# A two-layer adaLN and FFN kernel on one core: first w12 rows loaded and turned earlier, other orders of VectorE's and ScalarE's work, fewer self-waits

## What is computed

```python
x = x + L0_ffn(L0_cond(x, cond, ...), gate, kernel, bias, lora_A, lora_B, ...)
x = x + L1_ffn(L1_cond(x, cond, weight, c_weight, fside), w12, b12, w3, b3)
# L0_cond: a 64x64 mixing matrix per batch row, a softmax blend of eight
# L0_ffn:  x @ kernel + bias + two LoRA terms (one gated per group, one shared)
# L1_cond: a grouped conv over the 1024 positions (9 taps, 4 groups of 16 channels) + ctx + bias
# L1_ffn:
x12 = einsum('bsk,mk->bsm', x, w12) + b12        # w12: 2048 x 1024
x1, x2 = split(x12, 2)
x4 = silu(x1) * x2
return einsum('bsm,nm->bsn', x4, w3) + b3        # w3: 1024 x 1024
```

## Time and profile before

| what | us |
|---|---|
| the three timed runs | 838.28, 838.53, 830.34 |
| their median | 838.28 |
| the profiled execution, its own time | 831.89 |
| its span, first to last instruction | 829.8 |
| TensorE's mean granted clock in it | 0.985 of full speed |

### The profile page before, as it was taken

One profiled execution on the slowest core, in us unless ns is written; L12 is line 12 of the kernel. 1 busy time (PEld: TensorE's weight loads), 2 busy tenths in 40 slices (PEclk: granted clock), 3 DMA queues, 4 the chain that ended last, 5 costly groups with the idle time before them and its releaser, 6 DMA issues.

```text
span 829.8 us, 10413 instructions
## 1 busy us (share of the span) xinstructions
PE 786.4 (95%) x3889; PEld 659.2 (79%) x3889; DVE 532.7 (64%) x634; ACT 208.1 (25%) x251; POOL 88.3 (11%) x59
## 2 busy tenths in 40 slices
PE   5998889999999999789999999999999989999998
PEld 4867678888888999668888877877778868888886
DVE  4855775264443479987777759766665795565552
ACT  4431101010010032233333326332233641111110
POOL 4440532323222000000000000000000000000000
PEclk9999999999999999899999999999999999999999
DMA  8966845455455896244455232277754764444441
GB/s 277 238 180 188 216 109 132 122 119 135 111 143 127 199 279 194 70 126 127 126 159 145 76 127 77 64 200 206 203 163 177 271 236 152 153 152 152 167 161 76
DMA packets 88379, 131.45 MB, mean 158 GB/s; under 512 B 11208, under 2 KB 66936, under 8 KB 85656
## 3 DMA queue, kind: packets, MB, share of 16 engines
q1 hardware_dynamic: 85136, 129.90, 53.4%
q10 hardware_dynamic: 3064, 0.90, 0.7%
q0 software_dynamic: 144, 0.21, 0.1%
HBM read 78.20 MB, written 51.72 MB: 157 GB/s over the span
## 4 chain that ended last, share of the span: by engine, by line
PE 72%; DVE 10%; DMA 8%; SPq 5%; issue 3%; ACT 2%; DVEq 0%; ACTq 0%
PE ps L1561 30%; PE ps L1804 25%; PE ps L1862 16%; DMA w_raw<-in_L_ffn_w 2%; DVE cr L1279 1%; DVE cf L1271 1%; SPq L438 1%; DMA w_scratch<-w_d 1%; SPq L592 1%; DMA x<-x_scratch 1%; DVE w_s_lo L1252 1%; DMA lora_b_scratch<-lb_c_lo 1%; DMA h_f<-h_scratch 1%; SPq L355 1%; DMA res<-r_scratch 1%
## 5 line engine op out<-in xcount | busy, mean ns | idle before, releaser
L1804 PE MATMUL ps<-cr,w_s_hi 128*128 128x512 f32 x512 | 159.5, 393 | 5.1 <-ACT s L915 4.9
L1804 PE MATMUL ps<-cr,w_a_hi 128*128 128x512 f32 x384 | 122.2, 400 | 10.7 <-DVE s L1357 6.0
L1804 PEld LDWEIGHTS ps<-cr,w_s_hi 128*128 128x128 f32 x512 | 96.5, 189 | 27.2 <-issue 4.0
L1804 PE MATMUL ps<-cr,w_s_lo 128*128 128x512 f32 x256 | 100.2, 391 | 0.0
L1804 PEld LDWEIGHTS ps<-cr,w_a_hi 128*128 128x128 f32 x384 | 73.3, 192 | 28.4 <-DVE s L1357 8.1
L1561 PE MATMUL ps<-wk_hi,y_hi 128*128 128x512 f32 x256 | 80.5, 395 | 0.3 <-issue 0.3
L1561 PE MATMUL ps<-wk_lo,y_hi 128*128 128x512 f32 x256 | 79.0, 390 | 0.0
L1561 PE MATMUL ps<-wk_hi,y_lo 128*128 128x512 f32 x256 | 78.9, 389 | 0.0
L1127 DVE TENSOR_TENSOR x_t<-ps,x_t 128x1024 f32<-128x1024 f32 x16 | 19.6, 1222 | 92.3 <-PE ps L1561 92.3
L741 POOL TENSOR_TENSOR x_t<-x_in,f_bias 128x1024 f32<-128x1024 f32 x16 | 63.3, 3960 | 143.0 <-DMA x_scratch<-x_t 143.0
L1499 DVE TENSOR_TENSOR res<-ps,res 128x512 f32<-128x512 f32 x56 | 38.6, 689 | 59.0 <-PE ps L1862 58.3
(11 more groups left out here) (176 smaller groups left out, 1255.4 us busy)
## 6 DMA issues: line engine op xcount, KB each, us to landing
x_scratch<-x_t SPq DMA_DIRECT2D x128, 64.5 KB, 2.1
x<-x_scratch SPq DMA_DIRECT2D x32, 258.0 KB, 7.4
x_in<-in_x SPq DMA_DIRECT2D x16, 512.0 KB, 5.3
r_scratch<-r_t SPq DMA_DIRECT2D x16, 512.0 KB, 3.1
raw<-in_L_ffn_w SPq DMA_DIRECT2D x64, 128.0 KB, 4.7
h_scratch<-s SPq DMA_DIRECT2D x32, 256.0 KB, 2.4
h_f<-h_scratch SPq DMA_DIRECT2D x8, 1024.0 KB, 5.9
res<-r_scratch SPq DMA_DIRECT2D x16, 512.0 KB, 5.0
```

Source lines behind the costliest of these rows:

```text
L1804: last = pe.matmul(o, l, r, start=first and q == 0 and n == 0, stop=q == 3 and n == 2, skip_group_check=True)
```

## The change

- The first two w12 loads (prep 0) go to two buffers of their own (`raw_first`, over `la_hi`, free once GpSimd has gathered it) and are issued ahead of `store_x1` of tile 12. VectorE turns them behind the conv's rows 0 and 2, where it was rows 7 and 8, and sums and splits prep 0 earlier. SP's other issues in the conv get a new order (`load_c_bias(1)`, `store_a(0)`, the wait for the stores of r).
- VectorE's sums and low parts of c in the conv stand in another order; c_lo of t3 comes ahead of rows 29 to 31. The self-wait and `c_staged` in `take_c` go; SP waits for `c_taken` itself. TensorE waits for 29 rows ahead of b21 and for all 32 ahead of b22.
- ScalarE's order in a unit: `part_copy` 1 is ahead of the first silu; in units 9 to 14 `a_hi` is ahead of `part_copy` 0.
- Pass change: the operand t1 of pass B gets a new slot 16 (199.75 KB), so that VectorE's `c_sum` for it waits for no product; ScalarE's `silu` stands behind `part_copy` 1 there. raw2 moves to 24 KB, slot 3, its load for unit 9 waits for unit 7's b21.
- Units 9 to 14: `a_lo` is ahead of `s_lo`, w3's turns and first two differences are ahead of `part_add` 1 and the other two behind it. SP's `load_a` is ahead of `store_w3` and waits only for the two `a_lo`.
- Projection head: VectorE makes add 1 and add 2 ahead of the last w3 low part, and h of unit 1 behind add 3.

The diff, cut to what the text speaks of:

```diff
+        SLOT_KB = [8 * n for n in range(16)] + [199.75]
...
-        raw2 = at("w_a_raw", [P, 2, PH, P], 199.75)
+        raw2 = at("w_a_raw", [P, 2, PH, P], 24)
+        raw_first = [at(f"raw_first{s}", [P, NL], 64 + 4 * s) for s in range(2)]
...
-        T3, B22 = operand("t3", 48, 24), operand("b22", 56, 32)
+        T3, B22 = operand("t3", 48, 199.75), operand("b22", 56, 32)
...
-        LO_B, HI_B = dict(zip(PRODUCTS, (14, 1, 5, 3, 4, 12, 8))), dict(zip(PRODUCTS, (13, 9, 6, 7, 15, 10, 11)))
+        LO_B, HI_B = dict(zip(PRODUCTS, (14, 1, 5, 16, 4, 12, 8))), dict(zip(PRODUCTS, (13, 9, 6, 7, 15, 10, 11)))
...
             def load_w12(n):
                 for half in range(2):
-                    if n:
+                    if n > 1:
                         sp.wait_ge(w_free, 2 * n + half - 1)
                     for q in range(4):
-                        dst = raw[half][32 * q:32 * q + 32, :].rearrange("b (m l) -> b m l", m=4)
+                        dst = (raw if n else raw_first)[half][32 * q:32 * q + 32, :].rearrange("b (m l) -> b m l", m=4)
...
                 if n == HALF_UNITS:
-                    sp.wait_ge(w_free, 2 * HALF_UNITS)
+                    sp.wait_ge(g_mm, 7 * HALF_UNITS - 5)
                     sp.wait_ge(a_stored, 16 * (NJ - 2))
                 else:
-                    sp.wait_ge(w_lo_made, 4 * n)
+                    sp.wait_ge(w_lo_made, 4 * n - 2)
...
+            sp.wait_ge(la_gathered, NG)
+            load_w12(0)
             store_x1(TILES - 4, 0, TILES - 1)
             store_x1(TILES - 3, 1, TILES)
...
-            load_c_bias(1)
             for s in range(2):
                 sp.wait_ge(x1_stored[s], 128 * TILES // 2)
             load_x8(4)
             load_x8(5)
+            def store_c(k):
+                sp.wait_ge(c_taken, 8 + 16 + k + 1)
+                sp.dma_start(c_dram[k // 8, :, k % 8, :], c_st[k % 4][:, :]).then_inc(c_stored[k % 4], 16)
+            for t in range(6, 9):
+                load_x8(t)
+            store_a(0)
+            load_x8(9)
+            load_c_bias(1)
+            for t in range(10, 12):
+                load_x8(t)
             for s in range(2):
                 sp.wait_ge(r_stored[s], 16 * TILES // 2)
-            load_w12(0)
-
-            def store_c(k):
-
-                sp.wait_ge(c_staged, k + 1)
-                sp.dma_start(c_dram[k // 8, :, k % 8, :], c_st[k % 4][:, :]).then_inc(c_stored[k % 4], 16)
-
-            for t in range(6, 12):
-                load_x8(t)
-            store_a(0)
             load_w12(1)
...
-                if u == HALF_UNITS - 2:
-                    load_a(HALF_UNITS)
                 if u == HALF_UNITS - 1:
                     sp.wait_ge(g_mm, 7 * u + 1)
                     for s in range(4):
                         sp.wait_ge(c_stored[s], 16 * 4)
                     load_c(1, LO_B["b22"])
                     load_c(0, LO_B["b21"])
+                    load_a(HALF_UNITS)
                 if u == HALF_UNITS:
                     sp.wait_ge(g_mm, 7 * u)
                     load_w3_raw(0)
+                if 9 <= u <= 13:
+                    load_a(u)
                 if 9 <= u <= 12:
                     store_w3(u - 9)
-                if 9 <= u <= 13:
-                    load_a(u)
                 if 9 <= u <= 11:
...
+                if u > HALF_UNITS:
+                    act.wait_ge(g_mm, 7 * u)
+                    if n is not None:
+                        a_hi(n, 0)
+                        a_hi(n, 1)
+                    part_copy(u, 0)
+                    if n is not None:
+                        s_hi(n, 0)
+                        s_hi(n, 1)
+                    part_copy(u, 1)
+                    silu(u, 0)
+                    part_copy(u, 2)
+                    silu(u, 1)
+                    return
                 part_copy(u, 0)
-                if n is not None:
-                    a_hi(n, 0)
-                    a_hi(n, 1)
+                a_hi(n, 0)
+                a_hi(n, 1)
+                part_copy(u, 1)
                 silu(u, 0)
-                part_copy(u, 1)
-                if n is not None:
-                    s_hi(n, 0)
-                    s_hi(n, 1)
+                s_hi(n, 0)
+                s_hi(n, 1)
                 part_copy(u, 2)
...
             part_copy(U7, 0)
-            silu(U7, 0)
             act.wait_ge(g_mm, 7 * U7 + 2)
             c_hi_part(14, HI_B["b11"])
             part_copy(U7, 1)
+            silu(U7, 0)
+            part_copy(U7, 2)
             act.wait_ge(c_sum_made, 4 + 1)
-            act.wait_ge(g_mm, 7 * U7 + 4)
-            part_copy(U7, 2)
             c_hi_part(LO_B["t1"], HI_B["t1"])
...
-                dve.wait_ge(c_taken, 8 + b + 1)
-                dve.sem_inc(c_staged, 1)
             dve.wait_ge(xb_made, TILES)
             dve.wait_ge(u_mm, TILES + 4)
             dve.wait_ge(c_bias_loaded[0], 16)
-            for b in range(8):
-                take_c(b)
+            take_c(0)
             turn_w12(0, 0)
+            take_c(1)
+            take_c(2)
+            turn_w12(0, 1)
+            take_c(3)
...
             hidden_a(U7 - 1)
-            dve.wait_ge(g_mm, 7 * U7 + 2)
             c_sum(LO_B["t1"], 15, 14)
...
                 hidden_a(u - 1)
                 weight_sums(n)
+                a_lo(n, 0)
+                a_lo(n, 1)
+                s_lo(n, 0)
+                part_add(u, 0)
+                s_lo(n, 1)
                 if k is not None:
                     turn_w3(k, 0)
-                part_add(u, 0)
+                    turn_w3(k, 1)
+                    w3_sums(k, 0)
+                part_add(u, 1)
                 if k is not None:
-                    turn_w3(k, 1)
-                s_lo(n, 0)
-                s_lo(n, 1)
-                if k is not None:
-                    w3_sums(k, 0)
                     w3_sums(k, 1)
-                a_lo(n, 0)
-                part_add(u, 1)
-                a_lo(n, 1)
                 part_add(u, 2)
                 hidden_b(u)
...
             hidden_a(U15)
             add(0, 0, 0, 32)
             w3_lo_part(4)
+            w3_lo_part(5)
             add(0, 0, 1)
-            w3_lo_part(5)
+            add(0, 0, 2)
             w3_lo_part(6)
+            add(0, 0, 3)
+            dve.wait_ge(h_loaded[1], 16)
+            h_sums(1, 1)
+            add(0, 0, 4)
+            h_lo_tile0(1, 1)
+            add(0, 0, 5)
+            h_lo_tile1(1, 1)
+            h_lo_sums(1, 1, 0)
+            add(0, 0, 6)
+            h_lo_sums(1, 1, 1)
...
                 if c_first == 0:
-                    pe.wait_ge(c_taken, 8 + NB)
+                    pe.wait_ge(c_taken, 8 + 29)
                 gate_product(w, a12, slots, "b21", True)
                 c_ready(3)
                 pe.wait_ge(part_copied, u * 3 + 1)
@@ -1837,6 +1866,8 @@
                 pe.wait_ge(part_copied, u * 3 + 2)
                 gate_product(x, w3_, slots, "t3", False)
                 c_ready(6)
+                if c_first == 0:
+                    pe.wait_ge(c_taken, 8 + NB)
                 pe.wait_ge(part_copied, u * 3 + 3)
```

47 lines of the change are left out of this document (26 added, 21 removed).

## The result

The changed kernel takes 804.1 us (median of four runs: 802.3, 802.83, 805.36, 805.47) beside 836.95 of the kernel before in the same comparison (830.34, 835.63, 838.28, 838.53). The ratio is 0.9642, with a 95% interval from 0.9605 to 0.9679: it is faster. The profiled execution took 802.3, its span is 800.2. I had said 804, from 798 to 815. The total fits, but partly by luck: two of the terms under it do not, and a part of the program that the change does not speed up happened to be 4.0 us shorter.

A forecast was written before the change was run, and what follows sets the result against it. TensorE was taken as the bound, busy 95% of the span, with some 32 us open. Gains 2.1 + 11.2 + 3.2 + 8.5 + 5.0 = 30.0 from 831.9 gave 801.9; with 2 us for slips, 804, range 798 to 815.

The forecast's parts named there:

- Pass change: Units 7 and 8: new orders and t1's own slot keep VectorE ahead of TensorE, gaining 3.2 us (bounds 1.5 to 3.2).
- w3 units: Units 9 to 12: part_add 1 comes ahead of its bank and raw2 lands in time, gaining 8.5 us.
- projection: First projection unit: with add 1 and add 2 earlier nothing is late, gaining 5.0 us.
- Conv: Conv: the 1.57 us DMA gap and two small waits for emptied banks go, gaining 2.1 us.
- Unit 0: First unit behind the conv: takes 20.7 us instead of 31.9, a gain of 11.2.
- b22's gap of 1.6: Unit 0: new 1.6 us gap ahead of b22, as table load, silu and both s_hi precede part_copy 2.
- the 0 that I took: Unit 0: clock loss behind b22's new gap, taken as 0 us out of 0 to 1.9.
- The w3 units stay as they were: Rival, units 9 to 12: w3's raw quarter is the true bound, 6 of 8.5 us stay, total 810; chance 0.13.
- the change does little: Rival: ScalarE's copies behind turns bound unit 0, gaps only move, half of the 30 us stays, total 817; chance 0.05.
- DMAs in the conv: Rival: c_bias, sharing DMAs with store_a and x8 loads, lands late and delays row 31; total 810.5, chance 0.1.
- The slower rival: Rival, conv: store_a(0) waits for late w12 and holds x8 load 9 on SP; say 845 us, chance 0.02.
- The rule against the row: Skill rules against trace rows: self-waits' 2.6 us stay or go; unit 0's table load leaves a gap of 3.0 or 1.6.

The follow-up runs named there:

- e8: Changed kernel with ScalarE's and VectorE's old orders at the pass change, t1's new slot kept: units 7 and 8 take 41.24 us, ratio 0.9736.
- e7: Changed kernel with VectorE's old order in the projection's head: first projection unit takes 24.17 us, ratio 0.9744.
- e6: Changed kernel with VectorE's order in units 9 to 14 put back near the old one, both a_lo still first: units 9 to 12 take 76.16 us, ratio 0.9686.
- e5: Changed kernel with SP's load_a behind store_w3 again, waiting for all four low parts: units 9 to 12 take 82.35 us, ratio 0.9814.
- e1: Changed kernel with VectorE's two a_lo of prep 0 moved behind conv row 14: unit 0 takes 25.87 us, ratio 0.9668.
- e2: Changed kernel with SP's store_a(0) ahead of x8 load 6 instead of behind load 8: unit 0 takes 23.69 us, ratio 0.9635.
- e9: Changed kernel with store_a(0) ahead of x8 load 6 and two more c_st buffers: unit 0 takes 22.49 us, ratio 0.9645.
- e10: As e9, with unit 0's copies earlier on ScalarE and part_add 1 ahead of s_lo on VectorE: unit 0 takes 19.14 us, median 802.61, ratio 0.9639.
- e11: Changed kernel with prep 0's w12 loaded at its old place on SP, turns kept early: conv takes 63.81 us, ratio 0.9769.
- e4: Changed kernel with VectorE's 16 self-waits of the conv put back: unit 0 takes 28.82 us, ratio 0.9728.
- e3: Changed kernel with unit 0's order alone changed: part_copy 1 and 2 earlier on ScalarE, part_add 1 ahead of s_lo on VectorE; unit 0 takes 21.57 us, ratio 0.9652.

## Why the prediction was right and wrong

- **Pass change, w3 units, projection (3.2, 8.5, 5.0): right in size** (3.17, 8.56, 4.98), and e8 and e7 bear out the first and the last: with the old orders the old gaps come back. They were forecast as "what the stage loses against 19.04 us a unit", after a walk down VectorE's list showed nothing late. In the w3 units the reason was half wrong. I gave `part_add` 1's place and raw2's load together; e6 shows that once the load is early the place of the w3 work is worth nothing, and e5 that without the early load the new lists lose more than the old ones (10.5 us for 8.6), by way of ScalarE's order, which I had not gone through. I also had the raw quarter's landing as what is late next, with a wait of 1.5 a unit; it was 0.18 in unit 10 and none in units 11 and 12, and none in e6, where the turn stands 5.1 us into unit 10 and not 8.1. The work that I added up for such a unit is 14.7, not 14.5, which changes nothing.
- **Conv (2.1): mis-sized.** It gave 3.08. My own end of the conv, 336.3, would already have given 2.5, so the sum and the walk did not agree. The gaps of 1.57, 0.31 and 0.18 went as said, 2.06 together; the other 1.0 is that the four pieces into which the gaps cut the conv add up to 58.36, and one piece takes 57.33 (I had 57.6, from 192 records).
- **Unit 0 (11.2): the step that failed is the walk down VectorE's list in the conv**, "row 31 done at 337.0", that is 0.7 behind the conv's end of 336.3. It was 5.3 behind. The walk counted work and waits for banks, and left out what these instructions wait for in DRAM: `a_lo` for `store_a(0)`, which SP issues behind five x8 loads (5.68), and, once that is gone, row 20 for the store of row 16 (3.35 in e1, 3.73 in e2). In the kernel before, `a_lo` stood behind row 14, 2.2 us behind the landing of that store, so the trace of before showed no such wait. The change moved the store and `a_lo` up, `a_lo` further, and so made one. With the store ahead of the loads and two more buffers row 31 comes 2.4 and 1.0 late (e9, e10). From there the rest of the working holds: t3 "just in time" became 3.43 late, and b22's gap of 1.6 is there with 1.41 in e6, e9 and e11. In the changed kernel's own profile it does not show, because the clock fell behind t3's gap and t3 itself took as long (4.42 us) as ScalarE needed. That a gap of 1.4 costs no clock, the 0 that I took, held in e6 and e11 (1.00). The fall behind 565.08, which I took as the other bound, is not in the earlier trace rows; the window from 565 to 570 of the kernel before has 0.66.
- **The 4.02 ahead of the conv: not forecast, and, as far as the profiles show, no gain of the change.** The twelve profiles with this front part (the changed kernel and e1 to e11, the last without the early w12) have the conv start between 274.65 and 284.00, on average at 278.7, and the two with the old one at 278.67 and 278.00. The changed kernel's is the earliest of all. It happened to make up for unit 0, and that is luck. Without it, the change is worth 25.6 us by the traces where I had 30.0, and the sum would have come to 806.3 instead of 801.9; the 2 us that I had left for slips cover half of the difference. The medians say 33, but the kernel before had 831.6, 832.4 and 834.2 in the three later comparisons, so that 836.95 was on the high side.
- **The rivals.** "The w3 units stay as they were" and "the change does little" did not come true. "DMAs in the conv" had the right place and the wrong transfer: `c_bias` landed at 303.9, ahead of the 308 at which it is needed. The slower rival, SP's in-order queue with `store_a(0)`, had the right two instructions the wrong way round: x8 loads held the store, not the store a load. Its own price, a late first w12, was measured by e11 at 6.7 us in the conv.
- **The rule against the row.** For the self-waits the row won, though its 2.6 was low (e4: row 31 came 3.3 us later). For the table load too: 346.89 plus 1.28 is 348.17, and the ACTIVATE starts at 348.19, so nothing of the 1.38 us that the Trainium skill ("ScalarE: Activation LUTs", "What ACT_TABLE_LOAD costs") adds is seen, as in the earlier trace rows.

Left open: what makes the time ahead of the conv vary. The profiles differ there in waits for the LoRA blocks' DMAs (for `lora_b_scratch` none in the changed kernel, 3.0 in e2) and in stretches at the lower clock (in e3 the granted clock is 0.94, 0.91 and 0.91 up to 60, 100 and 140 us, in the changed kernel 1.00, 0.91 and 1.00), but no run was made to part them. It is not only the chip: e1 to e4, on one chip, start the conv between 275.43 and 284.00. Whether e10's 6.6 us can be had in the median is open as well; it was run once, beside three others.

## What to carry to other kernels

When an instruction is moved up in an engine's list, list everything it waits for, transfers included, and ask when each is issued on the queue of its own: a wait that was never seen can be made by the move. When one wait is removed, look for the next in the same chain before counting its gain; here a ring of four buffers hid behind it. And a load moved ahead in an in-order queue needs its condition moved too, or everything behind it pays (23 us here). An order that costs nothing while its input is on time can cost when it is not: with raw2 late, `a_hi` ahead of the copy lost 10.5 us (e5).

## What the runs showed that I had not expected

- The granted clock does not follow from the gap. Behind the same gap ahead of t3 (3.38 to 3.43 us) it fell to 0.77 and 0.89 in the changed kernel, to 0.74 and 0.58 in e1 and to 0.73 and 0.93 in e5, and stayed at 1.00 in e6 (340 to 365 us) and in e11 (355 to 365). Unit 0 was hardly longer for it (25.30 and 24.88), since the slower t3 covers the gap ahead of b22.
- The same code ahead of the conv took from 274.65 to 284.00 us, over 3% of it, in profiles whose undisturbed units agree to a few hundredths (19.04 to 19.06).
- A store of one row of c (128 x 256, one DMA) issued at 308.9 in e2 landed at 318.8, 9.8 us later, with the x8 loads and w12 of prep 1 underway; the same stores from 324 on took 1.8 to 1.9. A ring of four rows at 1.8 us each (57.1 for 32) covers 7.
